# A fused attention and expert kernel on one core: the query and key loads of the next tile moved ahead of the store of sums on SyncE's queue

## What is computed

```python
fq = jax.nn.elu(q) + 1.0
fk = jax.nn.elu(k) + 1.0
kv = jnp.einsum('bhnd,bhne->bnde', fk, v)
qkv = jnp.einsum('bhnd,bnde->bhne', fq, kv)
qk = jnp.einsum('bhnd,bnd->bhn', fq, fk.sum(axis=1))
attn = qkv / (qk[..., None] + 1e-06)
x = q_x + (attn @ wo + bo)
h = jax.nn.gelu(_ln(x, ln2_w, ln2_b) @ fc_w + fc_b, approximate=False)
return x + (h @ proj_w + proj_b)
...
pooled = x.mean(axis=1)
logits = pooled @ gate_w.T + gate_b
...
expert_out = jax.nn.gelu(jnp.einsum('bsd,eod->beso', x, expert_w) + expert_b[None, :, None, :], approximate=False)
return jnp.einsum('be,beso->bso', gates, expert_out)
```

## Time and profile before

| | |
|---|---|
| median of 3 runs | 1363.65 us (1358.73 to 1365.55) |
| the profiled execution: its own time | 1359.37 us |
| its span | 1357.6 us |
| PE busy | 1103.3 us (81%) |
| PEld busy | 807.2 us (59%) |
| DVE busy | 791.9 us (58%) |
| ACT busy | 527.6 us (39%) |
| POOL busy | 191.7 us (14%) |
| SyncE's transfers (q1) | 158.79 MB, 47.5% of 16 engines' span |
| ScalarE's transfers (q10) | 10.50 MB, 4.5% |

### The profile page before, as it was taken

One profiled execution on the slowest core, in us unless ns is written; L12 is line 12 of the kernel. 1 busy time (PEld: TensorE's weight loads), 2 busy tenths in 40 slices (PEclk: granted clock), 3 DMA queues, 4 the chain that ended last, 5 costly groups with the idle time before them and its releaser, 6 DMA issues.

```text
span 1357.6 us, 21399 instructions
## 1 busy us (share of the span) xinstructions
PE 1103.3 (81%) x7272; PEld 807.2 (59%) x7272; DVE 791.9 (58%) x1692; ACT 527.6 (39%) x835; POOL 191.7 (14%) x113
## 2 busy tenths in 40 slices
PE   5666969697887869898997869899898869596947
PEld 3344847475665648475765648576766548374723
DVE  2546556556665646766666646666666645565333
ACT  3313433435352524435362524536363514141422
POOL 1010202020202012121202012121202011111000
PEclk9756988989797979889897969889897979797969
DMA  4929091827374561919284561918375661902113
GB/s 167 211 69 224 33 195 46 182 89 163 108 143 129 137 152 63 223 48 209 92 180 124 137 151 63 208 63 188 114 162 140 145 143 47 163 17 70 47 62 109
DMA packets 150356, 170.17 MB, mean 125 GB/s; under 512 B 9104, under 2 KB 132240, under 8 KB 141840
## 3 DMA queue, kind: packets, MB, share of 16 engines
q1 hardware_dynamic: 143632, 158.79, 47.5%
q10 hardware_dynamic: 6656, 10.50, 4.5%
HBM read 93.75 MB, written 75.50 MB: 125 GB/s over the span
## 4 chain that ended last, share of the span: by engine, by line
PE 46%; DMA 23%; SPq 9%; issue 9%; DVE 7%; ACT 4%; ACTq 1%; DVEq 0%; POOL 0%; POOLq 0%
DMA kq<-scratch_k 14%; PE pq L957 12%; PE pj L943 10%; PE ps L919 8%; SPq L375 5%; PE pt L928 4%; PE pq L865 4%; DMA scratch_nd<-ot 3%; DMA scratch_v<-feat_v 3%; PE pt L853 2%; SPq L364 2%; DVE am L696 2%; DMA b_e<-in_eb 2%; ACT hidden L537 1%; SPq L387 1%
## 5 line engine op out<-in xcount | busy, mean ns | idle before, releaser
L957 PE MATMUL pq<-hT,w_fc 128*128 128x512 f32 x768 | 225.9, 434 | 9.8 <-DVE hT L719 6.2
L919 PE MATMUL ps<-kq 48*128 48x128 f32 x1024 | 144.2, 414 | 106.8 <-DMA kq<-scratch_k 83.0
L712 DVE TENSOR_TENSOR hidden<-xhT,hidden 128x512 fp32r<-128x512 f32 x128 | 100.5, 786 | 216.5 <-ACT hidden L537 216.3
L943 PE MATMUL pj<-w_pj,hidden 128*128 128x256 f32 x1536 | 214.5, 289 | 0.7 <-DVE hidden L712 0.7
L536 ACT ACTIVATE xhT<-pq,col 128x512 f32<-128x512 f32 x128 | 88.0, 687 | 320.8 <-PE pq L957 320.6
L919 PEld LDWEIGHTS ps<-kq 48*128 48x128 f32 x1024 | 122.5, 304 | 144.7 <-issue 130.2
L943 PEld LDWEIGHTS pj<-w_pj,hidden 128*128 128x128 f32 x1536 | 192.1, 189 | 18.6 <-issue 9.8
L696 DVE TENSOR_TENSOR am<-ps,mask 128x512 f32<-128x512 f32 x256 | 164.2, 682 | 57.9 <-PE ps L919 57.7
L957 PEld LDWEIGHTS pq<-hT,w_fc 128*128 128x128 f32 x768 | 149.7, 208 | 41.3 <-issue 7.4
L865 PE MATMUL pq<-zT,w_e 128*128 (+1 forms) x256 | 125.2, 639 | 47.1 <-DMA b_e<-in_eb 47.0
L865 PEld LDWEIGHTS pq<-zT,w_e 128*128 128x128 f32 x256 | 50.6, 206 | 104.6 <-issue 80.0
(11 more groups left out here) (117 smaller groups left out, 1415.5 us busy)
## 6 DMA issues: line engine op xcount, KB each, us to landing
kq<-scratch_q SPq DMA_DIRECT2D x96, 256.0 KB, 9.2
kq<-scratch_k SPq DMA_DIRECT2D x96, 256.0 KB, 15.3
scratch_q<-hidden SPq DMA_DIRECT2D x32, 512.0 KB, 10.7
scratch_k<-hidden SPq DMA_DIRECT2D x32, 512.0 KB, 4.9
scratch_nd<-ot SPq DMA_DIRECT2D x16, 1024.0 KB, 3.9
nd<-scratch_nd SPq DMA_DIRECT2D x48, 256.0 KB, 3.3
x_sb<-in_x SPq DMA_DIRECT2D x16, 512.0 KB, 3.8
scratch_v<-feat_v ACTq DMA_DIRECT2D x16, 512.0 KB, 19.5
```

The source lines that it names most:

```text
L712: nc.vector.tensor_tensor(hidden[:, m % SLOTS, 1], gelub[:, u], hidden[:, m % SLOTS, 0].bitcast(f32), ALU.subtract).then_inc(S["rest_ready ...
L919: last = nc.tensor.matmul(ps[j // 2][:, P * g:P * (g + 1)], group(kd, j, g), group(qd, j, g), start=True, stop=True)
L943: last = nc.tensor.matmul(pj[u][:, D * s:D * (s + 1)], hidden[:, m % SLOTS, a, lo:lo + P], w_pj[:, b, m], start=False, stop=end)
L957: last = nc.tensor.matmul(pq[m % 2][:, :], w_fc[:, b, c, P * m:P * (m + 1)], hT[:, a, c], start=(n == 0), stop=(n == len(order) - 1))
```

## The change

Two things are done. The stage `QK` is split into `QL` (six query loads) and `KL` (six key loads), and both are put right behind `M3`, in which the last scores are computed: ahead of `M4` with its store of sums, its numerator loads, and ahead of `VL`. And `XL`, the residual load, moves from behind `VL` to the beginning of the iteration, right behind `XS`. Nothing is computed otherwise; the lines from 381 on move up by one.

```diff
-LAG = {..., "QK": 1, "VL": 1, ...
+LAG = {..., "QL": 1, "KL": 1, "VL": 1, ...
...
-FULL = ["L", "XS", "M1", "J2", "Y", "M2", "DS", "M3", "Z", "D1", "M4", "VL", "XL", "QK", "X", "E", "J7", "F1", "N", "D2", "A2", "F3",
+FULL = ["L", "XS", "XL", "M1", "J2", "Y", "M2", "DS", "M3", "QL", "KL", "Z", "D1", "M4", "VL", "X", "E", "J7", "F1", "N", "D2", "A2", "F3",
         "FX", "R", "VT", "F2", "B0", "H", "B9", "JA"]
-HEAD = ["L", "XS", "M1", "J2", "Y", "M2", "DS", "M3", "Z", "D1", "M4", "VL", "XL", "QK", "E", "X", "J7", "G", "N", "D2", "F1", "A2",
+HEAD = ["L", "XS", "XL", "M1", "J2", "Y", "M2", "DS", "M3", "QL", "KL", "Z", "D1", "M4", "VL", "E", "X", "J7", "G", "N", "D2", "F1", "A2",
         "F3", "FX", "R", "VT", "F2", "B0", "H", "B9", "JA"]
...
-    "q_in": {"QK": 96}, "k_in": {"QK": 96}, "v_in": {"VL": 16 * NQ},
+    "q_in": {"QL": 96}, "k_in": {"KL": 96}, "v_in": {"VL": 16 * NQ},
...
-    stages(["DS", "D1", "VL", "QK", "X", "D2", "WS", "VT", "B0", "B9"], 1, [])
+    stages(["DS", "D1", "VL", "QL", "KL", "X", "D2", "WS", "VT", "B0", "B9"], 1, [])
...
-    stages(["XS", "C1", "J2", "C2", "Z", "C3", "C4", "XL", "J7", "E", "F1", "F3", "FX", "F2", "JA"], 18, [])
+    stages(["XS", "XL", "C1", "J2", "C2", "Z", "C3", "C4", "J7", "E", "F1", "F3", "FX", "F2", "JA"], 18, [])
...
-                if p.stage == "QK":
+                if p.stage in ("QL", "KL"):
+                    n, c, dst, parts = (0, "q", qd, Q_PARTS) if p.stage == "QL" else (1, "k", kd, K_PARTS)
                     for b in range(2):
                         wait(f"ps_full{b}", at(f"ps_full{b}"))
-                    for n, c, dst, parts in ((0, "q", qd, Q_PARTS), (1, "k", kd, K_PARTS)):
-                        wait(f"{c}_out", at(f"{c}_out"))
-                        for hf in range(2):
-                            for r, w in enumerate(parts):
-                                lo = 64 * hf + r
-                                sp.dma_start(dst[lo:lo + KP:len(parts)].bitcast(f32),
-                                             qk_dram[n][w, hf].rearrange("q (d h) t -> d q (h t)", h=H)
-                                             ).then_inc(S[f"{c}_in"], 16)
+                    wait(f"{c}_out", at(f"{c}_out"))
+                    for hf in range(2):
+                        for r, w in enumerate(parts):
+                            lo = 64 * hf + r
+                            sp.dma_start(dst[lo:lo + KP:len(parts)].bitcast(f32),
+                                         qk_dram[n][w, hf].rearrange("q (d h) t -> d q (h t)", h=H)
+                                         ).then_inc(S[f"{c}_in"], 16)
```

More of the change, by code:

```diff
@@ L37 @@
 DEN_EPS = 1e-6
-LAG = {"L": 0, "DS": 0, "D1": 0, "X": 0, "D2": 0, "QK": 1, "VL": 1, "VT": 1, "B0": 1, "B9": 1, "Y": 2, "N": 2, "A2": 2, "R": 2,
+LAG = {"L": 0, "DS": 0, "D1": 0, "X": 0, "D2": 0, "QL": 1, "KL": 1, "VL": 1, "VT": 1, "B0": 1, "B9": 1, "Y": 2, "N": 2, "A2": 2, "R": 2,
        "H": 2, "J7": 3, "JA": 3, "XS": 4, "J2": 4, "Z": 4, "E": 4, "F1": 7, "F3": 7, "FX": 7, "XL": 7, "F2": 7}
-FULL = ["L", "XS", "M1", "J2", "Y", "M2", "DS", "M3", "Z", "D1", "M4", "VL", "XL", "QK", "X", "E", "J7", "F1", "N", "D2", "A2", "F3",
+FULL = ["L", "XS", "XL", "M1", "J2", "Y", "M2", "DS", "M3", "QL", "KL", "Z", "D1", "M4", "VL", "X", "E", "J7", "F1", "N", "D2", "A2", "F3",
         "FX", "R", "VT", "F2", "B0", "H", "B9", "JA"]
-HEAD = ["L", "XS", "M1", "J2", "Y", "M2", "DS", "M3", "Z", "D1", "M4", "VL", "XL", "QK", "E", "X", "J7", "G", "N", "D2", "F1", "A2",
+HEAD = ["L", "XS", "XL", "M1", "J2", "Y", "M2", "DS", "M3", "QL", "KL", "Z", "D1", "M4", "VL", "E", "X", "J7", "G", "N", "D2", "F1", "A2",
         "F3", "FX", "R", "VT", "F2", "B0", "H", "B9", "JA"]
@@ L157, in walk @@
     first = ["L", "DS", "D1", "X", "D2"]
-    second = ["QK", "VL", "VT", "B0", "B9"]
+    second = ["QL", "KL", "VL", "VT", "B0", "B9"]
     late = ["XS", "J2", "Z", "E"]
```

## The result

| | before | after |
|---|---|---|
| median | 1361.19 us (4 runs) | 1526.57 us (4 runs, 1522.5 to 1527.75) |
| ratio, 95% interval | | 1.1229 [1.1189, 1.1269] |
| span of the profiled execution | 1357.6 us | 1525.9 us |
| granted clock, mean | 0.863 | 0.832 |

The change makes the kernel 12% slower, 165 us. The direction was forecast, the size was not: 1469 had been given, at most 1505.

A forecast was written before the change was run, and what follows sets the result against it. The landing of key loads was taken as the bound, with the path over the sums only 2.9 us behind. Ordinary iterations 12 x 9.5 = +114, choosing ones -3, clock -3: +108 us, forecast 1469 us, range 1400 to 1505.

The forecast's parts named there:

- The four signs: Changed profile: early loads land 20 us later, store takes 15 us, VectorE's numerator wait replaces TensorE's key wait, period about 81.
- Issue: On SyncE, twelve issues from T+0.1 (T: end of last scores) delay the store of sums from T+5.6 to T+7.8.
- Transfer: The twelve loads, 3.15 MB, moved ahead of the store: first lands at T+2.9, last at T+20.3 (T: end of last scores).
- The store lands 2.6 behind the last load: Store of sums, behind the loads on SyncE's queue, lands at T+22.9 instead of T+9.5 (T: end of last scores).
- The path behind: From the sums' landing 5.7 us to the division, 21.2 us more to `hn`'s end; nothing moved from `H` to next T.
- The clock: TensorE's granted clock in seven ordinary expert iterations: -0.5 us each, -3 in all, between -1 and +2.
- The reason given for the store's wait: Store of sums must wait for the loads ahead of it on SyncE's queue; only its latency is hidden.
- the store slips past: Rival: store of sums lands at about T+12.5 despite the loads, -40 us, 1323 us; chance 0.07.
- The choosing iterations: Three iterations that choose experts, adds of `A2` on VectorE: +1.4, about -1 and -3.3 us, together -3.
- `XL` "at nothing": Moving the residual load to the beginning of the iteration was set at no effect; its 0.35 us of issue matter little.
- worse: Rival: value loads, expert loads and idle clocks add to the chain, 13 us an iteration, 1525 us; chance 0.10.
- The 358 GB/s: Skill's HBM rate per core: loads would take 8.8 us, iteration 1 us longer; prediction used measured 158 GB/s instead.

The follow-up runs named there:

- experiment 7: Changed kernel with each of the twelve 256 KB loads laid out as 2 KB in each of 128 partitions (scores then wrong): 1344.9 us, 0.99.
- experiment 4: Changed kernel with the twelve loads issued by GpSimd at the same place, the store of sums staying on SyncE's queue: 1471.12 us, 1.0808.
- experiment 5: Changed kernel with the store of sums issued by ScalarE on its hardware queue, the twelve loads staying on SyncE's: 1459.83 us, 1.0722.
- experiment 1: Kernel before with only the residual load `XL` moved to the beginning of the iteration: 1350.61 us, 0.9922.
- experiment 11: Kernel before with only the order of the twelve loads changed, alternating between the two groups of partitions: 1309.4 us, 0.9613.
- experiment 3: Changed kernel with only two of the twelve loads ahead of the store of sums, ten behind `VL`, the residual load early: 1316.15 us, 0.967.
- experiment 6: Changed kernel with the store of sums put ahead of the twelve loads, the numerator loads still behind them: 1569.72 us, 1.1531.

## Why the prediction was right in direction and short in size

**That it is slower: right, by the path that was named.** The ceiling on the gain was small since the path behind the sums ends 2.9 us before `H` starts, and the store of sums became the late link. The four signs came: the wait for keys is gone, VectorE waits for the numerators (16.1 us in iteration 9), TensorE at line 998, and the store takes 18.8 us.

**Issue: nearly right.** The store went out at T+8.6, not 7.8; the first issue came at T+0.4.

**Transfer: the step that failed in size.** "The first lands at T+2.9 and the last at T+20.3" was built from the 17.4 us between the first and the last landing, with the 2.8 us of an empty queue ahead of them. Both were short. The 2.8 us are those of a numerator load, which goes to 128 partitions; on the queue that the change leaves empty the first of the narrow loads took 4.4 us, and the first wide one in experiment 7 took 2.7. And the twelve came 20.1 us apart, not 17.4, which was a low value: iterations 7 to 11 of before had 17.4 to 19.7. With the start at T+0.4 that makes T+24.8. From first issue to last landing the twelve took 644.60 - 621.08 = 23.5 us before and 715.99 - 691.58 = 24.4 after. The 23.5 stood in the rows. With it and the true start the last load would be in at T+23.9 and the store at T+26.5: 3.6 of the 4.3 us that the store was later than forecast, and 12 x 13.1 in place of 12 x 9.5.

**The store lands 2.6 behind the last load: right (2.4).** **The path behind: right.** 5.2 us from the landing to the division (5.7 forecast), 21.8 from there to `H` (21.2), and 31.0 from `H` to the next T, as before. The forecast shift of 9.5 us was the sum of right terms and one that was 4 us short; 14.0 came in iteration 9, 12.9 on the mean.

**The clock: it fell, where 3 us in all had been forecast as given back.** The mean granted clock fell from 0.863 to 0.832 and TensorE is busy 28 us longer; the projection's matmuls at line 998 take 396 ns in place of 314. It cost little: in iteration 9 the division to `H` is 0.6 us over the forecast, and from `H` to the next T nothing was lost.

**The reason given for the store's wait: right for the smaller part.** "A store waits for the loads ahead of it on SyncE's queue" explains 5 of 17.7 us (experiments 4 and 5). On the one queue the landing followed the order, 2.4 us behind the last load; what the prediction did not know is that without the order it would have been T+22 still. "ScalarE's store beside them isn't what makes them slow" was true, but that store's own 19.5 us on the page of before, for half a MB on a queue of its own, told what the loads do to others, and I did not use it. It also spoke against the rival "the store slips past", whose T+12.5 is 9 us short of the T+22 that was measured with separate queues.

**The choosing iterations: wrong.** A gain of 3 had been set against the ordinary ones; they lost 10. The adds came at T+48.5 in iteration 7, 3.5 us behind the forecast, where the store had landed 5.1 us behind it, at T+28.0.

**`XL` "at nothing": wrong,** 11 us by experiment 1, hidden in the change by the loads' new place.

**The rival "worse", 1525 by 13 us an iteration,** met the result to 2 us with a chance of 0.10. Its 13 us came from the 158 GB/s and a store 3.9 us behind; the measured row was 144 GB/s and 2.4. The two errors have opposite signs, so that it was met so closely is in part luck.

**The 358 GB/s** that the Trainium skill gives for a core ("DMA: Bandwidth & Descriptors", Specifications), set against the 158 in the prediction, were approached by the wide loads alone (326). With them the changed order comes out at 0.99 of before, but against the old order with the same loads it still costs 76 us.

## What to carry to other kernels

Before transfers are issued earlier, ask which transfer on the critical path is then in flight, on any queue: twelve slow loads held it nearly as long from another queue as the order of its own queue did, and giving it a queue of its own bought 5 us of 18. Time a batch of loads from its first issue to its last landing, not from its first landing. And look at how a load lies in SBUF before looking at when it goes out: two loops exchanged, so that successive loads write different halves of the partitions, gave 4% (experiment 11), where the best move in time gave 3% with the residual load's part in it (experiment 3).

## What the runs showed of the hardware that was not expected

- Loads of 256 KB into 16 partitions of one half fill the DMA engines (102.8%) at 144 GB/s; into 128 partitions they reach 326 GB/s at 100.6%. And beside the store, in experiment 4, the narrow loads kept 132 GB/s with 31.7% of the engines' time. A full engine is no sign of a full rate.
- A 1 MB store lands after 3.9 us alone and after 16.3 or 16.6 us beside twelve such loads that another queue carries; its first packet starts 0.8 us after the issue alone and 7.5 to 9.5 us beside them.
- SyncE's own issues took longer behind the store and the twelve loads in experiment 6: three took 7.89 us against 1.48 in the changed kernel, the next four 9.55 against 2.53. The prediction had taken issue time as fixed; what stretches it isn't shown, and one store's issue behind the same loads took 0.34 us.
- Six loads ahead of the store cost it 6.8 us of landing, twelve 14.9, two nothing.
- Not tried: the same writes with other reads, and loads of 2 KB pieces into 16 partitions, or of 8 KB pieces over both halves at once, which would tell the reading side, the size of the pieces and the number of partitions apart.
